# Two graph layers of a GNN kernel: each gather of the edge sums waits for the landing of the last but one

## What is computed

```python
def _L1_gnn_ref(x, edge_index, edge_attr, W, b):
    ...
    norm = dis[row] * w * dis[col]
    xw = x @ W
    msgs = xw[row] * norm[:, None]
    out = jax.ops.segment_sum(msgs, col, num_segments=n)
    return out + b

def _L3_gnn_ref(...):
    h = x @ W_in.T + b_in
    m = h @ W_msg
    agg = jax.ops.segment_sum(m[src], dst, num_segments=n_nodes)
    ...
```

## Time and profile before

| | us |
|---|---|
| Median of 3 timed runs | 5890.31 |
| Lowest and highest of them | 5886.95, 5895.29 |
| Span of the profiled execution | 6933.2 |
| of it GCN edge stage, about 2674 to 3868 | 1194 |
| of it GGN edge stage, about 5660 to 6834 | 1174 |

### The profile page before, as it was taken

The page is one execution under the profiler, slowest core; times in us unless marked ns, Lnnn a source line. Parts: engine busy times, 40 slices in busy tenths (PEclk is TensorE's granted clock), DMA queues, the critical chain, the costliest instruction groups (busy, mean ns, idle before and its releaser), DMA issues. The chain is left out here.

```text
span 6933.2 us, 103287 instructions
## 1 busy us (share of the span) xinstructions
PE 3719.0 (54%) x29332; PEld 3188.5 (46%) x29332; DVE 3593.0 (52%) x11040; ACT 1531.5 (22%) x3908; POOL 3988.6 (58%) x4360
## 2 busy tenths in 40 slices
PE   3555466555434452434454588888885853333436
PEld 1444355544333442334444477777774742223334
DVE  3278655587723343333344577777778951122225
ACT  0255200255300002000000244444442130000003
POOL 6366666266666645666666366666661455666662
PEclk8655577855566676555555799999997976566568
DMA  5266433366522223555564255555553731111111
GB/s 159 88 195 197 141 107 109 95 194 195 165 71 74 73 68 89 137 145 150 157 164 128 72 174 174 175 173 176 174 175 96 205 87 40 47 45 46 45 45 33
DMA packets 511394, 846.13 MB, mean 122 GB/s; under 512 B 116566, under 2 KB 220655, under 8 KB 510271
## 3 DMA queue, kind: packets, MB, share of 16 engines
q0 software_dynamic: 140576, 316.92, 17.7%
q1 hardware_dynamic: 210451, 305.33, 14.5%
q10 hardware_dynamic: 159840, 217.27, 10.8%
HBM read 654.62 MB, written 186.50 MB: 121 GB/s over the span
## 5 line engine op out<-in xcount | busy, mean ns | idle before, releaser
L2456 POOL DMA_INDIRECT s_rows<-rel_tab,src_v x832 | 786.6, 945 | 489.9 <-remote 280.7
L265 POOL DMA_INDIRECT stash<-gat_tab,src_g x784 | 750.9, 958 | 424.3 <-issue 167.4
L265 POOL DMA_INDIRECT gcn_rows<-gcn_tab,src_g x784 | 754.6, 963 | 416.2 <-issue 227.1
L265 POOL DMA_INDIRECT ggn_rows<-ggn_tab,src_g x784 | 744.2, 949 | 413.7 <-issue 224.8
L1621 PE MATMUL e_psb<-tmp,e_oh 128*128 x3328 | 639.7, 362 | 602.0 <-DVE e_oh L1589 391.1
L265 POOL DMA_INDIRECT stash<-in_x,src_g x732 | 705.8, 964 | 385.3 <-issue 154.6
L1621 PEld LDWEIGHTS e_psb<-tmp,e_oh 128*128 128x128 f32 x3328 | 575.2, 262 | 666.9 <-issue 666.4
L1954 PE MATMUL ggn_pso<-ggn_rows,ggn_oh 128*128 x1952 | 389.0, 374 | 693.1 <-issue 273.0
L1169 PE MATMUL g_psc<-g_parts,g_oh 128*128 128x52 bf16 x9408 | 480.5, 222 | 479.5 <-DVE g_oh L1088 260.7
L1954 PEld LDWEIGHTS ggn_pso<-ggn_rows,ggn_oh 128*128 128x128 f32 x1952 | 351.8, 274 | 731.0 <-issue 729.3
L1169 PEld LDWEIGHTS g_psc<-g_parts,g_oh 128*128 128x128 bf16 x9408 | 426.3, 120 | 534.3 <-DVE g_oh L1088 294.6
(11 more groups left out here) (507 smaller groups left out, 8609.8 us busy)
## 6 DMA issues: line engine op xcount, KB each, us to landing
g_lo_rows<-lo_rows ACTq DMA_DIRECT2D x392, 256.0 KB
oh_dram<-tmp ACTq DMA_DIRECT2D x208, 256.0 KB
s_oh<-oh_dram SPq DMA_DIRECT2D x208, 256.0 KB
edge_v<-acc SPq DMA_DIRECT2D x208, 256.0 KB
r_values<-edge_v SPq DMA_DIRECT2D x208, 256.0 KB, 2.9
edge_v<-stash SPq DMA_DIRECT2D x205, 256.0 KB
e_values<-edge_v SPq DMA_DIRECT2D x205, 256.0 KB
tmp<-drel_rows ACTq DMA_DIRECT2D x208, 128.0 KB
```

Source lines behind the costliest of these rows:

```text
L265: pool.indirect_dma_start(rows[:, t, :], None, tab[:, :], bass.IndirectOffsetOnAxis(ap=edges[:, t:t + 1], axis=0)).then_inc(s_land, 16)
L2456: pool.indirect_dma_start(rows[:, n % RING, t, :], None, rel_tab[:, :], bass.IndirectOffsetOnAxis(ap=src_v[:, n * GT + t:n * GT + t + 1], ...
```

## The change

`gather_rows` no longer calls `gather_group`. It issues the gathers itself, and each but the first two of a stage first waits until the gather two before it (`BEHIND = 2`) has landed. For this the landing semaphores are counted by tile of a group and no longer by slot of the ring: tile `t` of every group raises `s_tile[t]`, four semaphores instead of fourteen. At most two gathers are then in flight, so no two in flight raise the same semaphore. SP waits on all four for a group before it raises `s_landed`. No instruction changes its place on any engine. The sizes, tables, one-hots and sums are as before.

```diff
+BEHIND = 2
...
-        def gather_rows(pool, rows, tab, s_row, s_used):
+        def gather_rows(pool, rows, tab, s_tile, s_used):
 
             for g in range(GROUPS):
                 k = g % SLOTS
...
                     pool.wait_ge(s_used, n + RING)
                 pool.sem_inc(s_turn, 1)
-                gather_group(pool, rows[:, k, :, :], tab, src_g[:, g * GT:(g + 1) * GT], s_row[k])
-
-        def announce(sp, s_row, s_landed):
+                for t in range(GT):
+                    n = g * GT + t - BEHIND
+                    if n >= 0:
+                        pool.wait_ge(s_tile[n % GT], (n // GT + 1) * 16)
+                    pool.indirect_dma_start(rows[:, k, t, :], None, tab[:, :],
+                                            bass.IndirectOffsetOnAxis(ap=src_g[:, g * GT + t:g * GT + t + 1], axis=0)).then_inc(s_tile[t], 16)
+
+        def announce(sp, s_tile, s_landed):
 
             for g in range(GROUPS):
-                sp.wait_ge(s_row[g % SLOTS], (g // SLOTS + 1) * (16 * GT))
+                for t in range(GT):
+                    sp.wait_ge(s_tile[t], (g + 1) * 16)
                 sp.sem_inc(s_landed, 1)
...
-                s_row = landed("ggn_e")
+                s_row = landed("ggn_e", GT)
...
-                s_row = landed("gcn")
+                s_row = landed("gcn", GT)
```

## The result

The changed kernel takes **6413.9 us** (median of 4 runs, 6403.8 to 6415.9) against 5892.8 us for the kernel before (median of 4 runs, 5887.0 to 5897.3): **+521 us, ratio 1.0886, 95% interval 1.087 to 1.0901**. The sign of the forecast was right, its size was not: +110 us was predicted, and 6414 us lies 184 us above the end of the range.

The account below looks back on a forecast made before the run. In both stages POOL was taken as busiest, its gathers 1.25 us apart plus stalls for PE's held signals. The terms 24 + 70 + 15 = 109 us took the median from 5890 to 6000 us, range 5720 to 6230.

Parts of the forecast that it names:

- The base: GCN and GGN stages, first to last gather start: 1161 and 1149 us; terms added unscaled to the 5890 us median.
- held signals: Both stages: PE's signals seem held while gathers stream, so POOL stalls for 181 and 169 us.
- (b): New wait in the GCN stage: landing of 3.1 us, 1.57 us a gather, +70 us, bounds -20 and +423.
- (a): New wait in the GGN stage: landing 2.5 us plus 0.04 us, 1.28 us a gather, +24 us, bounds +16 and +35.
- (c): POOL's sequencer may lose its lead over the gathers: +15 us in GGN, nothing in GCN; bounds 0 and 143 us a stage.
- (d): SP waits on four semaphores instead of one, up to 588 more instructions of 17 ns a stage: zero.
- (e): Pacing's worth to PE's signals: gather stream stays unbroken, so held signals and 169 us of GGN stalls stay: zero.
- Faster: Rival: with two gathers in flight PE's signals come through and POOL's stalls go; -138 us, 5750 us, chance 0.35.
- another 140 us: Further gain in the rival Faster if GCN landings shrink to 2.6 us as well.
- No change: Rival: landing times fit the pace or the wait never binds in timed runs; 5890 +- 12 us, chance 0.10.
- Much slower: Rival: GCN landing stays at 3.6 us (+266), a quarter of POOL's lead lost in GGN (+35); +325, 6215 us.
- additions close behind PE's products: Sign that the forecast is wrong: DVE additions follow PE's products within 1 us throughout.

Follow-up runs that it names:

- the free stage: GCN stage with the gathers of the kernel before, without a window; that kernel, unchanged and profiled again, took 5885.7 us, this stage 987.4 us.
- the depth of 8: The changed kernel with BEHIND at 8 instead of 2 and eight landing signals instead of four, in both stages: 5888.0 us, ratio 1.0002 to the kernel before.

## Why the prediction failed, step by step

**The base.** The forecast took the stages as 1161 and 1149 us, from a profile 1043 us longer than the runs it stood for. It said that this was open, and that "If the held signals belong to the profile alone, the timed kernel is at POOL's free pace already, and any landing over 2.5 us costs in full". That sentence turned out true, and the sum hadn't been made by it. With 987 and 982 us as the base and the forecast's own paces of 1.57 and 1.28 us (1231 and 1004 us), the sum would have been 244 + 22 + 15 = +281 us, 6171 us, inside the range but still 243 us short of the measured time. The base is the largest single error: 171 of the missing 411 us. The step that failed beside it is (b), the GCN landing, with 407 - 244 = 163 us. Then comes (a) with 121 - 22 = 99 us, and (c) gave 15 us too many. By the stages this makes 171 + 163 + 99 - 15 = 418 us, against 411 timed.

**(a) The GGN wait, +24.** Measured +121 to +139. The landing of 2.5 us was right. The 0.04 us for the release was wrong. The row was of the first gather of a relation group, which follows the turn and carries no wait of its own (only the three behind it do), so it could not give the price of one. Where a gather stands waiting, it starts 0.18 us after SP's announcement of the same landing (median). Some 25 longer intervals add 30 us. The Trainium skill ("DMA: Bandwidth & Descriptors", section "Anatomy of one DMA — SWDGE (gpsimd) path") gave an estimate of 2.15 us and so no cost. No run here agrees: SP sees the landing 2.5 us after the start, the start-to-start time with one in flight is 2.80 us, and the trace was rightly preferred.

**(b) The GCN wait, +70, bounds -20 to +423.** Measured +407 to +426 against the free stage. The pace is 1.78 us where 1.57 was taken, that is 3.56 us for two gathers where the forecast had 3.14. The value near the lowest landing of three was the wrong choice, and the middle one (3.6 us, 1.82) would have given 1427 us, against 1394 measured. Three rows were also too few: the same profile has 196 such landings, with a mean of 3.7 us and a median of 3.4. The reason given, that a landing gets shorter with fewer gathers in flight, was right in its direction and too strong in its size. From the start of a group's last gather to SP's announcement pass on average 4.21 us in the free stage, 3.22 with two in flight and 2.68 with one. In the quiet GGN stage the same time is 2.57 to 2.65 us at every depth, so it is not the gathers behind one another alone that lengthen it. What delays landings is mainly the bursts of other transfers, and with one in flight the stage still takes 3.14 us a gather. The windows had shown them as a DMA share of 0.52 against 0.17, but as an average over bursts.

**(c) POOL's lead, +15.** Nothing of it was seen. In GGN the intervals ahead of a group's first gather, where a lost lead would show, hold 23 us above the free pace, fewer than those ahead of its other gathers (32, 27 and 42). The sequencer keeps its lead: the turn stands 0.91 us ahead of the group's first gather (median of the GGN stage), in the changed kernel as in the kernel before, profiled again. So the 0.77 us that the forecast took for a lost lead is no sign of one.

**(d) SP's waits, 0.** Confirmed by the depth of 8.

**(e) Held signals let stand, 0.** The term fell with its ground: there were no stalls in the timed runs, so none could stay or go.

**The rivals.** "Faster" (0.35) rested on the held signals and was void. Its "another 140 us" is also a slip: at landings of 2.6 us the pace is 1.32 us, 1035 us for the stage, 110 less than the 1145 before it. "No change" (0.10) had named a wait that never binds in the timed runs. It binds in both stages. "Much slower" at 6215 us had the right mechanism, waits that bind at both stages, and too low a price, because it too was laid on the stretched base. Of the signs named ahead, additions close behind PE's products came true (at most 1.3 us in the changed kernel), but as a sign that the stalls had never been in the timed runs. The Trainium skill's page "NOTIFIC — the notification-queue block", section "3. Interfaces", had given the ground for doubt. The runs show that the holding comes and goes between two profiles of one kernel. They don't show that this block causes it.

## What to carry to other kernels

Before anything is read from a profile, hold its span against the median of the timed runs. Where they differ by 18%, take no stage length and no stall from it, or make the sum on both bases and let the range hold both. A limit on transfers in flight costs nothing only if depth x issue pace exceeds the landing time plus the release of the waiter, and in a stage with bursts that is the landing inside a burst, not the average one. An average DMA share of 0.4 to 0.5 can be a share of 0.55 to 0.89 for some ten microseconds and of 0.2 in between.

## What the runs showed of the hardware

- A gather of 128 rows of 512 B that waits for another one's landing starts about 2.7 us after that one's start: in the GGN stage of the changed kernel the median is 2.73 us and the shortest 2.63 us, and with one in flight the median is 2.77 us. Of this 2.5 us pass until SP sees the landing and 0.2 us until the waiting gather starts. Issued without waits, one follows another in 1.25 us.
- A wait that is already met has no price that the runs can tell: with a depth of 8 every gather carries one, and the ratio is 1.0002.
- In one profiled execution PE's signals came up to 55 us late in the GCN stage, and it ran 18% longer than the timed runs. A second profile of the same kernel showed none of it. The cause is left open.
- Side transfers of the same bytes weighed unequally: two loads of 128 KB spread from one row cost the waiting gathers about 200 us in the stage, a store of 256 KB about 64 us (185 and 48 against the changed kernel's own stage). The loads' packets are of 1 KB, the store's of 2 KB. Over the windows after step 16 the rings' busy time (share x length) falls from 0.42 x 1310 = 550 us to 0.36 x 1263 = 455 without most of the store and to 0.33 x 1124 = 371 without most of the loads. So the loads take nearly twice as much of the rings, but delay by three to four times as much. Why is left open.
